# Experts' choice as a lane of its own, the causal second pass refilled, and a new order for a two-block transformer kernel

## The reference

```python
x = x + diag_attention(layernorm(x))        # softmax over the queries, only its diagonal times V
x = x + local_block(layernorm(x))           # 2 layers: 8 heads of 64, windows of 64 looking one window back,
                                            # l2-normed and rotated q and k, then LN, gated GELU FFN
x = x + causal_attention(layernorm(x))      # 16 heads of 8
scores = softmax(x_ @ gate_w)               # x_ = layernorm(x); 8 experts
topk_w, topk_idx = top_k(scores, 2); topk_w = topk_w / (sum(topk_w) + 1e-20)
y = sum_e w_per_expert[:, e] * (silu(x_ @ w_gate[e]) * (x_ @ w_up[e])) @ w_down[e]
x = x + y + shared_expert(x_)
```

## Time and profile before

| | |
|---|---|
| runs before | 1705.53, 1713.02, 1709.93 us; median 1709.93 us |
| profiled execution | 1709.73 us, its span 1708.0 us |
| PE busy | 1532.9 us, 90% of the span, 11632 products |
| DVE busy | 1233.1 us, 72% |
| ACT busy | 965.7 us, 57% |
| POOL busy | 600.9 us, 35% |
| mean granted clock of TensorE | 0.977 of full speed |

### The profile page before, as it was taken

The page is one execution under the profiler, slowest core; times in us unless marked ns, Lnnn a source line. Parts: engine busy times, 40 slices in busy tenths (PEclk is TensorE's granted clock), DMA queues, the critical chain, the costliest instruction groups (busy, mean ns, idle before and its releaser), DMA issues.

```text
span 1708.0 us, 29745 instructions
## 1 busy us (share of the span) xinstructions
PE 1532.9 (90%) x11632; PEld 908.0 (53%) x11632; DVE 1233.1 (72%) x2636; ACT 965.7 (57%) x1786; POOL 600.9 (35%) x401
## 2 busy tenths in 40 slices
PE   5779987899998999888999999988998889988999
PEld 2444553545565555645556465554555445645556
DVE  5877878776688657985588856886669547885544
ACT  3475765456654766548745577448653553662451
POOL 1866836152071612625044430716106115110000
PEclk8999999899999999999999999999999999998999
DMA  4200000310160101601024100421016002504102
GB/s 140 68 2 22 23 7 22 75 24 1 44 135 17 24 10 52 124 10 24 19 67 108 25 2 29 112 54 24 11 37 140 3 1 69 118 3 106 46 10 69
DMA packets 37293, 80.13 MB, mean 47 GB/s; under 512 B 6783, under 2 KB 22655, under 8 KB 33777
## 3 DMA queue, kind: packets, MB, share of 16 engines
q1 hardware_dynamic: 37152, 78.22, 19.1%
HBM read 54.74 MB, written 8.78 MB: 37 GB/s over the span
## 4 chain that ended last, share of the span: by engine, by line
PE 30%; DVE 9%; ACT 8%; issue 2%; POOL 2%; POOLq 0%; DVEq 0%; ACTq 0%
PE ps L500 27%; DVE bsmall L1346 2%; ACT work L957 2%; PE ps L505 2%; ACT bigs L1040 2%; DVE fsmall L1219 1%; POOL work L1497 1%; DVE fsmall L1211 1%; ACT L1066 1%; POOL fsmall L1476 0%; DVE work L1182 0%; ACT bigs L1066 0%; ACT L1002 0%; POOL work L1508 0%; DVE x L1436 0%
## 5 line engine op out<-in xcount | busy, mean ns | idle before, releaser
L1476 POOL TENSOR_TENSOR fsmall<-fsmall,consts 128x8 f32<-128x8 f32 (+1 forms) x140 | 201.5, 1452 | 200.9 <-DVE fsmall L1115 193.2
L1497 POOL TENSOR_TENSOR work<-work 128x1024 f32<-128x1024 f32 x56 | 137.0, 2447 | 379.9 <-DVE work L1182 379.8
L500 PE MATMUL ps<-bxt,mw 128*128 128x512 f32 x504 | 251.1, 605 | 6.0 <-DVE bigs L1448 4.2
L500 PE MATMUL ps<-maskb,identb 128*128 128x128 bf16 (+1 forms) x1152 | 228.7, 239 | 19.3 <-ACT work L957 15.1
L957 ACT ACTIVATE work<-ps,fsmall 128x128 f32<-128x128 f32 x448 | 164.5, 510 | 44.0 <-DVE fsmall L1223 43.6
L1346 DVE TENSOR_REDUCE bsmall<-ps 128x1 f32<-128x512 f32 (+3 forms) x308 | 177.5, 632 | 14.6 <-PE ps L500 14.2
L1040 ACT ACTIVATE bigs<-ps 128x512 f32<-128x512 f32 x280 | 151.9, 652 | 29.7 <-PE ps L500 29.0
L500 PE MATMUL ps<-wqkv,h 128*128 128x512 f32 x336 | 159.5, 601 | 9.2 <-ACT vs L917 5.5
L505 PE MATMUL ps<-ident,work 128*128 128x128 f32 x924 | 133.5, 285 | 32.6 <-ACT work L957 15.6
L1528 POOL TENSOR_TENSOR work<-work,fsmall 128x1024 f32<-128x1024 f32 x56 | 106.1, 1896 | 150.9 <-DVE fsmall L1214 150.9
L1066 ACT ACTIVATE bigs<-ps 128x512 f32<-128x512 f32 x126 | 75.1, 597 | 139.1 <-PE ps L500 138.3
(11 more groups left out here) (337 smaller groups left out, 3005.8 us busy)
## 6 DMA issues: line engine op xcount, KB each, us to landing
mw<-in_experts SPq DMA_DIRECT2D x63, 384.0 KB, 3.2
pks<-scr_partsb SPq DMA_DIRECT2D x42, 192.0 KB
pqs<-scr_partsb SPq DMA_DIRECT2D x126, 64.0 KB
v2s<-vs SPq DMA_DIRECT2D x14, 512.0 KB, 4.4
v2s<-vs SPq DMA_DIRECT2D x14, 384.0 KB, 5.8
scr_partsb<-bigs SPq DMA_DIRECT2D x7, 768.0 KB, 3.7
wqkv<-in_experts SPq DMA_DIRECT2D x9, 384.0 KB, 3.1
out<-x SPq DMA_DIRECT2D x7, 256.0 KB, 12.0
```

The source lines that it names most:

```text
L500: return nc.tensor.matmul(o, a, b, start=start, stop=stop, skip_group_check=True)
L1476: return nc.gpsimd.tensor_tensor(out, x, consts[:, k:k + 1].broadcast_to([x.shape[0], x.shape[1]]), op)
L1497: nc.gpsimd.tensor_tensor(R.qk[:, m, :], R.qk[:, m, :], R.part[m % 2], ALU.add).then_inc(R.l_add.sem, 1)
```

## The change

What it does, part by part:

1. The choice of experts becomes a fifth lane, R, for sequences 0 to 6: `route` leaves `back`. The expert products no longer stand behind it; what waits for its result is the addition of the first expert (`r_w`). PE's first expert product waits for the turned rows itself. For `back7` the order of the steps stays.
2. The second causal pass fills its ten slots in another order, and the weighing is released by parts: part 0 needs 4 exponentials, part 2 needs 6, parts 1 and 3 need all ten. Parts 0 and 2 are issued behind fills 6 and 8 of their own group, parts 1 and 3 behind fill 1 of the next. An exponential of the next group waits only for the part that read its slot. The copy `oc` stands behind the next group's third exponential.
3. `embed` decides by the round: `fronts` uses one bank only from its second round on (`on_one_bank`).
4. `scale_rotary` is cut by layer: layer 0 behind the scores' maxima of sequence 0, layer 1 behind its second normalisation. SyncE waits for both before it loads experts over the staged tables.
5. `normalise` is issued as a scalar_tensor_tensor, its rstd as a broadcast tensor input, in place of a tensor_scalar with two pointers.
6. SyncE waits for an expert's down product only where a load follows.
7. All five order strings are new.

```diff
 ORDER = {
     "tensor": (
-        "BBEBEBEBEBEBEEEBBBBEBFFFFBFFBFFFFFFBFBFFFBBBFFBBBBBFFFFBFFFFBFFFFBBBFFFFFFBFBBFFBBFFBBFBFBFFFFBBBBBFFFFFBFBF"
+        "BEEEBEEEEBBBBBEFFBBBFBFFBFBFFFFBFFFFFBBFFFBFBFBBBBFBBFBFBFBFFBFFBBFBFBBBBFBBFFBFFFBFFFBBFFBFBBBFBFFFFBBFFFFFB"
...
-EXP_FILLS = [f for a in (0, 2) for f in ([(a, 0)], [(a + 1, 0)], [(a, 1), (a, 3)], [(a + 1, 1), (a + 1, 3)],
-                                         [(a, 2), (a + 1, 2)])]
+EXP_FILLS = [[(hd, 0)] for hd in range(4)] + [[(0, 2), (1, 2)], [(2, 2), (3, 2)]] + [[(hd, 1), (hd, 3)] for hd in range(4)]
+PV_ORDER = [0, 2, 1, 3]
+PV_NEEDS = {0: 4, 2: 6, 1: 10, 3: 10}
+PV_FREES = {0: 1, 2: 2, 3: 3}
+def freed_by(n):
+    return 1 if n < 4 else 2 if n < 6 else 3
...
+        def on_one_bank(R, s):
+            return R.beside and s > 0
+        def embed_banks(R, s):
+            return [R.fb[3]] * 4 if on_one_bank(R, s) else R.fb
...
+                def weigh(gg, kk):
+                    if kk == 0:
+                        if gg:
+                            pe.wait_ge(R.c_oc.sem, R.c_oc.at(s, gg))
                         else:
-                            pe.wait_ge(R.c_e.sem, R.c_e.at(s, k - 2))
...
+                            pe.wait_ge(R.c_mr.sem, R.c_mr.at(s, 2))
+                    pe.wait_ge(R.c_e.sem, R.c_e.at(s, 10 * gg + PV_NEEDS[kk]))
+                    for hd in range(4):
+                        slot, at = EXP_AT[(hd, kk)]
+                        i = mm(R.bb[3][32 * hd:32 * hd + 32, kk * P:T], R.va[:, kk, 4 * gg + hd, :],
+                               R.big[slot][:, at:at + T - kk * P], start=(kk == 0), stop=(kk == PV_ORDER[-1]))
+                    if kk in PV_FREES:
+                        i.then_inc(R.c_pv.sem, 1)
+                for gg in range(4):
+                    r, g = gg // 2, gg % 2
+                    for n in range(len(EXP_FILLS)):
+                        yield f"s{g}{n}.{r}"
+                        scores(r, g, n)
...
+                        if gg and n == 1:
+                            for kk in (1, 3):
+                                yield f"pv{(gg - 1) % 2}{kk}.{(gg - 1) // 2}"
+                                weigh(gg - 1, kk)
+                        if n in (6, 8):
+                            kk = n - 6
                             yield f"pv{g}{kk}.{r}"
...
+                            weigh(gg, kk)
+                for kk in (1, 3):
+                    yield f"pv1{kk}.1"
+                    weigh(3, kk)
...
+                if R is back7:
+                    yield from route(R, s)
+                yield from experts(R, s)
+            def route(R, s):
                 yield "route"
...
-                for r in range(2):
-                    for g in range(2):
-                        gg = 2 * r + g
-                        for n in range(len(EXP_FILLS)):
-                            yield f"s{g}{n}.{r}"
-                            if n == 0 and gg:
-                                act.wait_ge(R.c_pv.sem, R.c_pv.at(s, gg))
...
+                    for n in range(len(EXP_FILLS)):
+                        yield f"s{g}{n}.{r}"
+                        k = 10 * gg + n
+                        if gg:
+                            act.wait_ge(R.c_pv.sem, R.c_pv.at(s, 3 * (gg - 1) + freed_by(n)))
+                        act.wait_ge(R.c_s2.sem, R.c_s2.at(s, k + 1))
+                        nc.scalar.activation(R.big[n], R.bb[k % 3][:, :], ACT.Exp).then_inc(R.c_e.sem, 1)
+                        if gg and n == 2:
+                            yield f"oc{(gg - 1) % 2}.{(gg - 1) // 2}"
+                            keep_weighed(gg - 1)
...
-                    i = ts(xn[:, tt, :], src[:, tt, :], mv[:, tt, 0:1], rs[:, 1, tt:tt + 1], ALU.subtract, ALU.mult)
+                    i = stt(out=xn[:, tt, :], in0=src[:, tt, :], scalar=mv[:, tt, 0:1],
+                            in1=rs[:, 1, tt:tt + 1].broadcast_to([P, P]), op0=ALU.subtract, op1=ALU.mult)
...
-                if R is front0:
-                    scale_rotary()
...
+                if R is front0:
+                    yield "rotary0"
+                    scale_rotary(0)
...
+                if R is front0:
+                    yield "rotary1"
+                    scale_rotary(1)
...
                     dve.wait_ge(R.m_d.sem, R.m_d.at(s, e + 1))
+                    if e == 0:
+                        dve.wait_ge(R.r_w.sem, R.r_w.at(s, 1))
...
-                    sp.wait_ge(R.m_d.sem, R.m_d.at(s, e))
                     if e + SLOTS - 1 < ALL or not last:
+                        sp.wait_ge(R.m_d.sem, R.m_d.at(s, e))
                         load_expert(R, (e - 1 + SLOTS) % ALL)
```

327 lines of the change are left out of this document (164 added, 163 removed).

## The result

The changed kernel took 1703.05 us in the median of 20 runs (1696.66 to 1710.65). The kernel before, on the same chip, took 1709.68 us in the median of 20 (1703.44 to 1716.2). The ratio is 0.9967, with a 95% interval of 0.9952 to 0.9983: 0.33% or 6.6 us faster, certain as a gain, but less than half of the 15 us of the forecast and within the 0.5% that was called "same". The profiled execution took 1705.3 us; its span is 1703.5 us, against 1708.0 before.

A forecast was written before the change was run, and what follows sets the result against it. TensorE, working 1532.94 of 1708.00 us, was taken as the bound, leaving its idle time and lower clock to win. Start 5, second pass 8, choice 2, normalisation 0 and rest 0 make 15 us: 1709.9 to 1695 us, range 1673 to 1716.

The forecast's parts named there:

- likeliest case: Whole kernel: 1695 us, with its own range of 1685 to 1704 us, chance 0.43.
- likeliest of three signs: Whole kernel: faster than 1701.4 us at 0.60, slower than 1718.5 us at 0.13, the rest between at 0.27.
- The start: First pair of sequences: projecting earlier starts GpSimd's full stretch earlier, a gain of 5 us, bounds 0 and 9.
- The second pass: Causal second pass: new fills and weighing by parts remove 8 of 11.6 us of PE's waits, bounds 3 and 12.
- The choice: Choice of experts as a lane: less waiting for the first gated product, a gain of 2 us, bounds 0 and 4.
- The normalisation: Normalisation in another instruction: gain of 0, bounds -0.9 us and 5.2 us, what PE waited for it.
- The order: New order on all engines, mainly the middle: gain of 0, with bounds of 10 us either way.
- (a): Windowed exponentials queue behind ScalarE's nearly unbroken causal ones; PE's waits grow by 11 us: 1706 us, chance 0.25.
- (b): Each windowed tile behind a running causal pass waits one fill longer, 28 us in all: 1723 us, chance 0.12.
- (c): More than the parts: start 9, second pass 12, choice 4, new places 8, together 33 us: 1677 us, chance 0.2.
- (d): At the start GpSimd's full stretch and sequence 0 decide; 5 us don't come or 2.5 are lost: 1700 to 1703.
- must stay near 1533 us: Whole kernel, profile after: PE's work stays near 1533 us, while its idle time in the middle falls some 10 us.

The follow-up runs named there:

- 1: The changed kernel with the first two sequences' windowed steps and sequence 1's embedding back in the old order: 1709.73 us, ratio 1.0012 against the kernel before.
- 7: The changed kernel with the old tensor_scalar instruction in the normalisation: 1704.22 us, ratio 0.9976 against the kernel before.
- 9: The changed kernel run again, unaltered: 1699.33 us.
- 10: The changed kernel run a third time, unaltered: 1704.75 us.
- 11: The changed kernel with one GpSimd step, sequence 1's fourth division of probabilities, moved ahead of three steps of sequence 0: 1698.64 us, ratio 0.9938 against the kernel before.
- 3: The kernel before with only the new start (four banks, split tables, new order of the first steps): 1711.21 us, ratio 1.0028 against the kernel before.
- 8: The kernel before with only the start's code edits (four banks, split tables), in the old order: 1708.62 us, ratio 1.0002 against the kernel before.
- 13: The kernel before with the new start and one GpSimd step moved (sequence 1's fourth division of probabilities): 1708.59 us, ratio 1.0012 against the kernel before.
- 2: The changed kernel with the choice of experts put directly ahead of the first expert step on each engine: 1730.57 us, ratio 1.0131 against the kernel before.
- 6: The changed kernel with all four weighing parts together behind the next group's second fill, and the old order of fills: 1741.47 us, ratio 1.020 against the kernel before.
- 5: The changed kernel with its new fills, but all four weighing parts together behind the next group's second fill: 1719.79 us, ratio 1.0077 against the kernel before.
- 12: The kernel before with only the choice of experts as a lane of its own: 1728.86 us, ratio 1.0133 against the kernel before.

## Why the forecast was right or wrong

**The sum.** 15 us forecast, 6.6 measured. 1703.05 lies in the range of 1673 to 1716 us and at the upper edge of the likeliest case's own. The likeliest of three signs was "faster by over 0.5%", and it came out as "same". With the split at the first maximum most of the miss has one place: the rest of the kernel brought 8.2 us in the profiled execution, where the forecast had 10 (8 + 2). Over all traces with the changed kernel's later rounds intact (after, 1, 7, 9, 10, 11; 7 but for the normalisation's instruction) it is 1370.0 to 1377.9 us, against 1381.5 to 1386.1 in those with the old ones (before, 3, 8, 13), 9.5 us between the means. The start brought -3.7 us where the forecast had +5. That is 8.7 of the 10.5 us by which this pair of traces falls short of 15 (1708.0 to 1703.5 is 4.5). Beside this split runs a term that the prediction held at nothing: the changed kernel's mean clock is lower by 0.003, and among its own 20 executions 0.001 of clock goes with 1.0 us. By these two numbers some 3 us of the gain are lost to the clock, an estimate that no run tests.

**1. The start: the failing step.** Right were these: the bank waits gone, sequence 1 at 35.25 us, sequence 0 at 43.5, the one early and the other late. The step that failed is "so an earlier pair starts it earlier. I take 5 us", together with the sentence ahead of it on GpSimd. I took GpSimd's full stretch from 70 us on the earlier trace rows as a block of work that begins sooner. It is that, and a gate for VectorE besides: an instruction of 0.17 us that fell among three of GpSimd's back to back waited for all three. The prediction had the row for it: L1223 at 2125 ns against 168, and it even wrote that this line is stretched beside GpSimd. It used it only to value the normalisation's form. The bounds of the term, 0 to 9, left out a loss for this reason. The price, from the two kinds of traces with the same code: 316.1 and 318.8 us without the long product, 324.5 to 328.4 with it, over 5 us at least; and 319.3 us with the step moved. The 4.1 us of the stretch grow on the way: the eighth of GpSimd's divisions of probabilities (L1585) ends at 105.2 to 106.6 us in the long kind and at 102.2 to 103.4 in kernels 2, 6, 11 and 13, the twelfth at 172.5 to 173.8 and 163.8 to 167.0. Without it the start would have given 3.2 us (322.5 - 319.3), close to the forecast's 5. What makes the product come during the first or the second of GpSimd's pair stays open: the clock from 80 to 84 us is 0.50 to 0.70 in the long kind and 0.63 and 0.68 in the short one, and no run set it by itself. Kernel 11, at 0.50, shows that it needn't matter.

**2. The second pass: mis-sized in its rows.** "ScalarE needs 5.0 + 0.6 = 5.6 us a group, and PE's own work, 5.88 us in such a stretch, sets the pace" is wrong: a group takes 7.44 us, a quarter more. The window of 8 us in the earlier trace rows didn't hold a whole group; over one group PE works 6.9 to 7.05 us. So 0.74 us a group was there to win (8.18 to 7.44), not 2.1, and "I take 8 of 11.6" of the waits on L1040 did not come: 4.7 + 4.4 us stand where 4.9 + 6.7 stood, and all waits on that line went from 12.6 to 13.4 us. What the edit does instead is free ScalarE's queue for the windowed half: undone in the laid order it costs 17 us (5), of which 10.7 are waits on windowed exponentials, and with the old fills 38 us (6). What the term of 8 us brought by itself can't be told from the rest, so that the total came near is no merit of it.

**3. The choice.** In its row the term of 2 us was exact: the wait on the first gated product fell from 4.2 to 1.7 us. As a statement on the lane's worth it meant little, since the order was laid around it: 27 us to take it out (2), 23 to put it in alone (12).

**4. The normalisation** at 0: right, 1704.2 against 1703.1 us, both intervals overlapping, medians 3 ns apart (7). By the Trainium skill, "VectorE: DVE Perf Modes", "The perf-mode tier table (the rule you actually need)", an f32 tensor_scalar in SBUF runs at twice the rate of a tensor_tensor; the table has no row for scalar_tensor_tensor, which I had read as a tensor_tensor. Nothing of such a factor shows here: 344 and 341 ns. By the Trainium skill, "SBUF — State Buffer", "SBUF: two separate sides", an instruction with two SBUF inputs needs the port pair shared with GpSimd and is blocked while a GpSimd instruction that reads SBUF has it. The trace agrees in that the 128x8 product ends 0.02 us behind the end of a GpSimd instruction; that it waited for three of them, 4.30 us, is the measurement's own.

**5. The order** at 0 with 10 either way. It can't be separated. The rounds in the middle ran 4 to 20 us behind the kernel before (sequence 5's first fill at 1312.2 us against 1302.8), and came ahead within that sequence's causal step (its turning at 1388.3 against 1390.3), in which the new order has 7.7 us less of work for PE: 12 of 18 products `work,w` and 16 of 64 turnings of the windowed half stand elsewhere. PE's idle time in the middle fell by 9.5 us, as written ("some 10 us less"), but by waits on row maxima (11.8 to 6.9 us), on the gated product and on smaller ones, not by those named.

**The rivals.** (a) and (b) took their warning from waits on windowed exponentials beyond 33 and 45 us. Both figures start from the 21.7 us of the middle, and there the waits are 23.4 us: a sign for neither. Over the whole span they rose from 30.7 to 45.7 us (without those named pqs), but 13.3 of those 15 us stand before 322 us, where no second pass runs. Run 5 shows that the edit lowers them. (a)'s time, 1706, was nearer than mine, for a reason that it didn't have. (c) failed with the start and the second pass's size. (d), "the 5 us don't come, or 2.5 are lost", described the start nearly as it came, down to the suspect ("GpSimd's full stretch"), and I had put it inside the likeliest case at no chance of its own.

**PE's work "must stay near 1533 us":** 1539.2 in the profiled execution. For the same products it was 1530.0 us at a clock of 0.981 (11), 1539.2 at 0.970 and 1541.5 at 0.973 (7).
